# Feed-forward stages: block strides and reciprocals in PSUM, a shared bank, and the output product made later

## The chip, the cores and the metric

The kernel runs on one core of one Trainium2 chip. Times are microseconds of device time. A core has TensorE (PE, matrix products and transposes into PSUM), VectorE (DVE), ScalarE (ACT), GpSimd (POOL) and SyncE (SP), which issues DMAs. Each engine works its own list of instructions in order and waits on semaphores. PSUM has 8 banks of 512 float32 a partition here, and this stage uses them all.

## The reference

A network of two layers on 8 batches of 1024 tokens, 256 wide. Layer 0 is attention with relative positions, layer 1 is two Mamba layers, and each is followed by a feed-forward stage. The change touches only the two feed-forward stages, so this part of the reference matters:

```python
def fp4_quant_dequant(x):            # BLOCK = 16
    xb = x.reshape(shape[:-1] + (shape[-1] // BLOCK, BLOCK))
    scale = jnp.max(jnp.abs(xb), axis=-1, keepdims=True) / 6.0
    scale = jnp.maximum(scale, jnp.float32(1e-12))
    xn = xb / scale
    idx = jnp.searchsorted(_MID, jnp.abs(xn))
    q = _GRID[idx] * jnp.sign(xn) * scale
def fp4_linear(x, w):
    return jnp.einsum('bsk,nk->bsn', fp4_quant_dequant(x), fp4_quant_dequant(w))
gate = fp4_linear(x, w_gate)         # 256 -> 704
y = fp4_linear(x, w_up)
return fp4_linear(jax.nn.silu(gate) * y, w_down)   # 704 -> 256
...
h = _layernorm(x, axis=-1) * (1 + cb) + sb
x = x + gb * _L0_ffn_ref(h, L0_ffn_w_gate, L0_ffn_w_up, L0_ffn_w_down)
```

## The kernel before

`ffn_phase` (from L1298) does one feed-forward stage. It runs twice, over 64 tiles of 128 tokens each time. The quantised and turned weights stay in SBUF.

The loop is a software pipeline. `body(t, ...)` is called on every engine for t = n, and each part of it works on another tile: `early` on n+4 (mean and variance), `ahead` on n+3 (centering and modulation), `norm` on n+2 (rounding x to fp4), `turn` on n+1 (transpose of x, gate and up products), `middle` on n (h = silu(gate) * up, rounding h), `hturn` on n-1 (transpose of hq), `last` on n-2 (output product, gating, residual). The order of instructions on each engine is the order of the code in its body; no scheduler moves anything.

The names that matter, with their lines in the profile of before:

- TensorE, in this order: the output product into `out_ps` (L1673, six matmuls), two transposes of `xq` into `xT_ps` (L1682), six transposes of `hq` into `hT_ps` (L1692), eight gate and eight up matmuls into `gu_ps` (L1703). The transposes of `hq` wait for `s_hq`, which GpSimd raises.
- VectorE: `xamax` L1571, h L1578, `xstride` L1583, `hamax` L1587, `xinv` L1590, `hstride` L1593, `xq = xn * xinv` L1597, `xtmp` L1601, `hinv` L1604, statistics L1609, `hq = h * hinv` L1613, `htmp` L1622, the gating of the output L1627, then the four additions and subtractions that round: L1630 and L1632 on `xq`, L1635 and L1637 on `hq`.
- ScalarE: the copy of the turned x (L1739), centering (L1745), the masks' scaling (L1749, L1763), the copies of the turned `hq` (L1757, L1759), silu (L1770).
- GpSimd: modulation L1497 and L1503, `xscale` L1499, the residual add L1511, `hscale` L1513, the chain for the inverse deviation L1518, L1519, L1521, L1523, and last the scaling of `xq` and then `hq` by their block scales (both L118).

The strides and reciprocals (one number for each block of 16) lie in SBUF, `xT_ps` and `out_ps` have a PSUM bank each.

Of the kernel before, what the change touches and what calls it, by code (L numbers as in the profile page):

```python
# [15 lines left out]
P = 128  # L16
D = 256
# [10 lines left out]
FFN = 704  # L28
FC = -(-FFN // P)
BLOCK = 16  # L30
# [1267 lines left out]
def ffn_phase(nc, name, x_in, x_out, mods, w_gate, w_up, w_down, ident, batches):  # L1298
# [7 lines left out]
    with ExitStack() as ctx:  # L1306
        def sb(n, shape, dt=FP32):
            return ctx.enter_context(nc.sbuf_tensor(f"{name}_{n}", shape, dt))
# [44 lines left out]
        xq = sb("xq", [P, 2, D])  # L1353
        xtmp, htmp = sb("xtmp", [P, D]), sb("htmp", [P, FFN])
        xamax, hamax = sb("xamax", [P, 2, D // BLOCK]), sb("hamax", [P, 2, FFN // BLOCK])
        xstride, hstride = sb("xstride", [P, D // BLOCK]), sb("hstride", [P, FFN // BLOCK])
        xscale, hscale = sb("xscale", [P, D // BLOCK]), sb("hscale", [P, FFN // BLOCK])
        xinv, hinv = sb("xinv", [P, D // BLOCK]), sb("hinv", [P, FFN // BLOCK])
        xqT = sb("xqT", [P, 2, DC, P])
        gate = sb("gate", [P, 2, FFN])  # L1360
        h = sb("h", [P, FFN])
# [1 line left out]
        hqT = sb("hqT", [P, 2, FC, P])  # L1363
        res = sb("res", [P, 2, D])
        gu_ps = pb("gu_ps", [P, 4, BANK])
        xT_ps = pb("xT_ps", [P, BANK])
        hT_ps = pb("hT_ps", [P, 2 * BANK])
        out_ps = pb("out_ps", [P, BANK])

        turned_up = gu_ps[:, :, :].rearrange("p (c a) w -> p c (a w)", c=DC)  # L1370
        turned_down = gu_ps[:, 0:2, :].rearrange("p a w -> p (a w)")
# [268 lines left out]
        @block.tensor  # L1640
        def _(pe):
            def prepare(k):
                if k == 0:
                    return
                m = k - 1
                w = part(made, m)
                pe.wait_ge(s_wq, m + 1)
                ge(pe, s_wkept, m)
                if m < 2:
                    for c in range(FC):  # L1650
                        cw = min(P, FFN - c * P)
                        mm = nc.tensor.transpose(turned_down[0:cw, c * P:(c + 1) * P], w[:, c * P:c * P + cw], ident[:, :])
                elif m < 4:
                    for i in range(edge // P):
                        for c in range(DC):
                            mm = nc.tensor.transpose(turned_up[:, c, i * P:(i + 1) * P],
                                                     w[:, i * D + c * P:i * D + (c + 1) * P], ident[:, :])
                else:
                    for c in range(DC):
                        mm = nc.tensor.transpose(turned_up[:, c, 0:P], w[:, c * P:(c + 1) * P], ident[:, :])  # L1660
                mm.then_inc(s_wT, 1)
                if k == jobs:
                    pe.wait_ge(s_wkept, jobs)

            def body(t, early, ahead, norm, turn, middle, hturn, last):
                if last:
                    t0 = t.plus(-2)
                    k, u = t0.n, t0.u
                    pe.wait_ge(s_hqT, k + 1)
                    ge(pe, s_gated, k)  # L1670
                    for c in range(FC):
                        cw = min(P, FFN - c * P)
                        mm = nc.tensor.matmul(out_ps[:, 0:D], hqT[0:cw, u, c, :], wd[0:cw, c, :],  # L1673
                                              start=(c == 0), stop=(c == FC - 1))
                    mm.then_inc(s_out, 1)
                if turn:
                    t1 = t.plus(1)
                    k, u = t1.n, t1.u
                    pe.wait_ge(s_xq, k + 1)
                    ge(pe, s_xqT, k)  # L1680
                    for c in range(DC):
                        mm = nc.tensor.transpose(xT_ps[:, c * P:(c + 1) * P], xq[:, u, c * P:(c + 1) * P],  # L1682
                                                 ident[:, :])
                    mm.then_inc(s_xT, 1)
                if hturn:
                    t1 = t.plus(-1)
                    k, u = t1.n, t1.u
                    pe.wait_ge(s_hq, k + 1)
                    ge(pe, s_hqT, k)
                    for c in range(FC):  # L1690
                        cw = min(P, FFN - c * P)
                        mm = nc.tensor.transpose(hT_ps[0:cw, c * P:(c + 1) * P], hq[:, u, c * P:c * P + cw],  # L1692
                                                 ident[:, :])
                    mm.then_inc(s_hT, 1)
                if turn:
                    t1 = t.plus(1)
                    k, u = t1.n, t1.u
                    pe.wait_ge(s_xqT, k + 1)
                    ge(pe, s_h, k)
                    for w, at in ((wg, 0), (wu, 2)):  # L1700
                        for a in range(2):
                            for c in range(DC):
                                mm = nc.tensor.matmul(gu_ps[:, at + a, 0:HALF], xqT[:, u, c, :],  # L1703
                                                      w[:, c, a * HALF:(a + 1) * HALF],
                                                      start=(c == 0), stop=(c == DC - 1))
                        mm.then_inc(s_gate if at == 0 else s_gu, 1)
            run(pe, body, prepare)
# [831 lines left out]
```

## Time and profile before

| | |
|---|---|
| median of 3 runs | 9465.37 us (9464.44 to 9467.9) |
| the profiled execution | 9470.18 us, span 9468.5 us |
| the two feed-forward stages | about 3790 to 4430 us and 8790 to 9462 us of the span |
| steady part, TensorE / VectorE / GpSimd busy in 500 us | 475.8 / 494.3 / 425.9 us at a granted clock of 1.00 |

A stage begins with its weights and then settles to one tile after another. A row of a timeline or of the chain of waits shows the start in us from the start of the span, the duration in us, the engine, the line and what it writes and reads; in square brackets stands the idle time of the engine before it, and who ended it. A row of a line's durations shows the least, the median and the greatest in ns. Instructions of one engine overlap slightly at their ends, so the distance from start to start says more than the sum of durations.

### The profile page before, as it was taken

What the parts mean: (1) busy time and instruction counts of PE and PEld (TensorE: products, weight loads), DVE (VectorE), ACT (ScalarE), POOL (GpSimd) and SP (SyncE); (2) the same over time, 40 slices, a digit from 0 to 9 for tenths busy, and PEclk for the clock granted to TensorE, in tenths of its full rate; (3) what the DMA queues carried; (4) which work ended last, traced back from release to release, by engine and by line L of the source; (5) the groups of instructions that cost most, each with busy time, mean ns of one, the idle gap of its engine ahead of it and who ended that gap; (6) DMA issues with size and microseconds to landing.
All of it is one profiled execution on the core that took longest, in us unless ns stands there. A gap on an engine that the chain in (4) does not pass through costs nothing. (4 is left out here: it accounts for less than half of the span.)

```text
span 9468.5 us, 173659 instructions
## 1 busy us (share of the span) xinstructions
PE 8233.9 (87%) x48392; PEld 4721.2 (50%) x48392; DVE 8331.3 (88%) x12866; ACT 5642.4 (60%) x9235; POOL 5082.2 (54%) x4769
## 2 busy tenths in 40 slices
PE   6699999999999997897888888887788888888699
PEld 2366666666666666564333333333233333333466
DVE  5788888888888887997899999999699999999899
ACT  2377777777777775332666666665456656555333
POOL 1100000000000000785899999999699999999687
PEclk8799999999999999998999999999899999998899
DMA  7988888888888888111122111221222222211111
GB/s 236 306 272 281 282 280 283 281 281 279 282 283 281 280 280 267 46 43 47 77 82 82 72 56 77 82 82 44 94 80 72 76 91 91 91 68 71 53 43 40
DMA packets 1173912, 1447.40 MB, mean 153 GB/s; under 512 B 83402, under 2 KB 1053658, under 8 KB 1140736
## 3 DMA queue, kind: packets, MB, share of 16 engines
q1 hardware_dynamic: 1173568, 1444.18, 46.3%
q14 instruction: 295, 2.42, 0.1%
q8 instruction: 49, 0.80, 0.0%
HBM read 880.81 MB, written 564.60 MB: 153 GB/s over the span
## 5 line engine op out<-in xcount | busy, mean ns | idle before, releaser
L2109 POOL TENSOR_TENSOR mb_bx<-mb_dtu,mb_bc 128x512 f32<-128x512 f32 x2048 | 2662.0, 1324 | 13.7 <-DVE mb_hs L2209 13.2
L2352 PE MATMUL mb_y_ps<-mb_g,ident 128*128 128x512 f32 x4096 | 2187.1, 640 | 469.2 <-POOL mb_g L2116 235.0
L2396 ACT ACTIVATE mb_dA<-mb_dt,mb_a_neg 128x512 f32<-128x512 f32 x2048 | 1401.0, 688 | 1627.6 <-DVE mb_hs L2209 1084.9
L1471 POOL MEMSET f_magic<- 128x1 f32 x2 | 0.2, 98 | 3383.6 <-POOLq L127 3383.6
L2352 PEld LDWEIGHTS mb_y_ps<-mb_g,ident 128*128 128x128 f32 x4096 | 763.6, 199 | 1650.5 <-issue 729.0
L1017 ACT ACTIVATE at_tab<-at_e_ps 128x384 f32<-128x384 f32 x2064 | 1012.1, 490 | 790.1 <-PE at_e_ps L934 789.4
L1071 DVE TENSOR_REDUCE at_nmax<-at_s_ps 128x1 f32<-128x1024 f32 x1025 | 1255.2, 1225 | 35.1
L950 PE MATMUL at_pT_ps<-ident,at_probs 128*128 128x128 f32 x8192 | 1115.6, 279 | 101.8 <-ACT at_probs L1022 84.8
L1022 ACT ACTIVATE at_probs<-at_s_ps,at_nmax 128x1024 f32<-128x1024 f32 x1025 | 1140.8, 1113 | 62.5 <-DVE at_nmax L1071 39.0
L950 PEld LDWEIGHTS at_pT_ps<-ident,at_probs 128*128 128x128 f32 x8192 | 894.6, 141 | 403.2 <-ACT at_probs L1022 374.4
L2169 DVE TENSOR_TENSOR mb_g<-mb_hs,mb_bc 128x512 f32<-128x512 f32 x1472 | 993.7, 675 | 39.6 <-PE mb_y_ps L2352 38.3
L2209 DVE TENSOR_TENSOR_SCAN mb_hs<-mb_dA,mb_carry,mb_bx 128x512 f32<-128x512 f32 x736 | 935.4, 1283 | 98.0 <-POOL mb_bx L2109 38.2
L2209 DVE TENSOR_TENSOR_SCAN mb_hs<-mb_dA,mb_bx 128x512 f32<-128x512 f32 x736 | 896.5, 1224 | 77.2 <-POOL mb_bx L2109 38.1
L917 PE MATMUL at_s_ps<-at_opnd 105*128 105x512 bf16 (+3 forms) x2818 | 804.8, 326 | 9.2 <-DMA at_skew<-at_tables 8.8
L2116 POOL TENSOR_TENSOR mb_g<-mb_hs_sb,mb_bc 128x512 f32<-128x512 f32 x576 | 752.6, 1307 | 93.3 <-PE mb_y_ps L2352 85.3
L1069 DVE TENSOR_TENSOR at_s_ps<-at_s_ps,at_skew 128x384 f32<-128x384 f32 (+1 forms) x1025 | 542.8, 530 | 280.6 <-PE at_s_ps L921 157.1
L1076 DVE COPY at_probsT<-at_pT_ps 128x512 f32<-128x512 f32 x1024 | 697.0, 681 | 0.1
L969 PE MATMUL at_c_ps<-at_probsT,at_val 128*32 128x128 f32 x16384 | 659.7, 279 | 1.6 <-ACT at_probsT L1029 1.6
L921 PE MATMUL at_s_ps<-ident,at_skew 128*128 128x128 f32 x2818 | 609.2, 274 | 0.0
L2285 PE MATMUL mb_ring<-mb_xc,mb_diag 128*128 128x512 f32 x1024 | 522.7, 596 | 46.3 <-ACT mb_u L2449 43.7
L969 PEld LDWEIGHTS at_c_ps<-at_probsT,at_val 128*32 128x32 f32 x16384 | 384.9, 109 | 212.3 <-issue 202.0
L921 PEld LDWEIGHTS at_s_ps<-ident,at_skew 128*128 128x128 f32 x2818 | 392.4, 142 | 85.1 <-issue 0.4
(244 smaller groups left out, 14167.9 us busy)
## 6 DMA issues: line engine op xcount, KB each, us to landing
at_tables<-at_tab SPq DMA_DIRECT2D x1032, 384.0 KB, 4.0
at_skew<-at_tables SPq DMA_DIRECT2D x1030, 256.0 KB, 3.1
mb_bc<-mb_bc_rows SPq DMA_DIRECT2D x256, 1024.0 KB, 6.3
at_skew<-at_tables SPq DMA_DIRECT2D x773, 128.0 KB, 3.5
at_opnd<-at_q_st SPq DMA_DIRECT2D x130, 210.0 KB, 4.4
at_opnd<-at_kl_st SPq DMA_DIRECT2D x130, 210.0 KB, 4.7
at_opnd<-at_kr_st SPq DMA_DIRECT2D x130, 210.0 KB, 4.6
at_q_st<-st_parts SPq DMA_DIRECT2D x96, 256.0 KB, 4.1
```

The source lines that it names most:

```text
L917: mm = nc.tensor.matmul(s_ps[:, b, a * P:z * P], opnd[:, u, 0, q], opnd[:, u, side, a * P:z * P], start=True, stop=(len(near) == 0))
L921: mm = nc.tensor.matmul(s_ps[:, b, kt * P:(kt + 1) * P], skew[:, u, 1, kt, blk * P:(blk + 1) * P], ident[:, :], start=False, stop=(kt == n ...
L950: mm = nc.tensor.transpose(pT_ps[:, hb, k * P:(k + 1) * P], probs[:, i % 2, c:c + P], ident[:, :])
L969: mm = nc.tensor.matmul(c_ps[lane * VW:(lane + 1) * VW, q:q + P], val[:, h.u, k + lane, :], probsT[:, i0 % 2, (k + lane) * P:(k + lane + 1 ...
L1017: nc.scalar.activation(tab[:, e, :], e_ps[:, 0:BAND], ACT.Copy).then_inc(s_tab, 1)
L1022: nc.scalar.activation(probs[:, i % 2, :], s_ps[:, i % 2, :], ACT.Exp, bias=nmax[:, i % 2:i % 2 + 1], scale=1.0).then_inc(s_exp, 1)
L1071: nc.vector.tensor_reduce(nmax[:, b:b + 1], s_ps[:, b, :], axis=AX.X, op=ALU.max, negate=True).then_inc(s_max, 1)
L2109: pool.tensor_tensor(bx[:, s % RINGS, :], dtu[:, c, :], bc[:, 0, n, :], ALU.mult).then_inc(s_bx, 1)
L2169: nc.vector.tensor_tensor(g[:, s1 % RINGS, :], state(s1), bc[:, 1, n, :], ALU.mult).then_inc(s_g, 1)
L2209: nc.vector.tensor_tensor_scan(state(s), dA[:, s % DA_RING, :], bx[:, s % RINGS, :], initial=carry[:, s:s + 1] if k.u else 0.0, op0=ALU.mu ...
L2352: nc.tensor.matmul(y_ps[:, c % 2, :], ident[:, :], g[:, s1 % RINGS, :], start=False, stop=(n == STATE - 1)).then_inc(s_y, 1)
L2396: nc.scalar.activation(dA[:, s % DA_RING, :], dt[:, c, :], ACT.Exp, scale=a_neg[:, c, n:n + 1]).then_inc(s_dA, 1)
```

## The change

Three things change. The strides and reciprocals of the blocks of x and h move from SBUF to four quarters of a new PSUM bank, `blocks_ps`. To free that bank, `out_ps` and `xT_ps` become two halves of one bank, `out_xT_ps`, with two more waits that keep the engines from using both halves at once. And TensorE makes the output product behind the transposes of x and of `hq`, no longer ahead of them; the gate and up products stay behind it.

```diff
-        xstride, hstride = sb("xstride", [P, D // BLOCK]), sb("hstride", [P, FFN // BLOCK])
         xscale, hscale = sb("xscale", [P, D // BLOCK]), sb("hscale", [P, FFN // BLOCK])
-        xinv, hinv = sb("xinv", [P, D // BLOCK]), sb("hinv", [P, FFN // BLOCK])
...
-        xT_ps = pb("xT_ps", [P, BANK])
         hT_ps = pb("hT_ps", [P, 2 * BANK])
-        out_ps = pb("out_ps", [P, BANK])
+        out_xT_ps = pb("out_xT_ps", [P, BANK])
+        out_ps, xT_ps = out_xT_ps[:, 0:D], out_xT_ps[:, D:2 * D]
+        blocks_ps = pb("blocks_ps", [P, BANK])
+        xstride, xinv = (blocks_ps[:, i * BANK // 4:i * BANK // 4 + D // BLOCK] for i in (0, 1))
+        hstride, hinv = (blocks_ps[:, i * BANK // 4:i * BANK // 4 + FFN // BLOCK] for i in (2, 3))
...
             def body(t, early, ahead, norm, turn, middle, hturn, last):
-                if last:
-                    t0 = t.plus(-2)
-                    k, u = t0.n, t0.u
-                    pe.wait_ge(s_hqT, k + 1)
-                    ge(pe, s_gated, k)
-                    for c in range(FC):
-                        cw = min(P, FFN - c * P)
-                        mm = nc.tensor.matmul(out_ps[:, 0:D], hqT[0:cw, u, c, :], wd[0:cw, c, :],
-                                              start=(c == 0), stop=(c == FC - 1))
-                    mm.then_inc(s_out, 1)
                 if turn:
                     t1 = t.plus(1)
                     k, u = t1.n, t1.u
                     pe.wait_ge(s_xq, k + 1)
                     ge(pe, s_xqT, k)
+                    ge(pe, s_gated, k - 3)
...
                     mm.then_inc(s_hT, 1)
+                if last:
+                    t0 = t.plus(-2)
+                    k, u = t0.n, t0.u
+                    pe.wait_ge(s_hqT, k + 1)
+                    ge(pe, s_gated, k)
+                    if turn:
+                        pe.wait_ge(s_xqT, t.plus(1).n + 1)
+                    for c in range(FC):
+                        cw = min(P, FFN - c * P)
+                        mm = nc.tensor.matmul(out_ps[:, 0:D], hqT[0:cw, u, c, :], wd[0:cw, c, :],
+                                              start=(c == 0), stop=(c == FC - 1))
+                    mm.then_inc(s_out, 1)
```

TensorE's list for one tile in the loop of the first stage, before the change; a row shows the line, the operation, what it writes and reads, and the shape.

```order
L1673 MATMUL f_out_ps<-f_wd,f_hqT 128x256 x6
L1679 ISA
L1682 MATMUL f_xT_ps<-ident,f_xq 128x128 x2
L1692 MATMUL f_hT_ps<-ident,f_hq 128x128 x5
L1692 MATMUL f_hT_ps<-ident,f_hq 64x128
L1703 MATMUL f_gu_ps<-f_wg,f_xqT 128x352 x4
L1703 MATMUL f_gu_ps<-f_wu,f_xqT 128x352 x4
```

The same place after the change; L1696 is the output product, L1674 the transpose of x, L1684 that of `hq`.

```order
L1670 ISA
L41 REGISTER_ALU
L1674 MATMUL f_out_xT_ps<-ident,f_xq 128x128 x2
L1684 MATMUL f_hT_ps<-ident,f_hq 128x128 x5
L1684 MATMUL f_hT_ps<-ident,f_hq 64x128
L1696 MATMUL f_out_xT_ps<-f_wd,f_hqT 128x256 x6
L1707 MATMUL f_gu_ps<-f_wg,f_xqT 128x352 x4
L1707 MATMUL f_gu_ps<-f_wu,f_xqT 128x352 x4
```

The output product of tile n-2 now stands behind the transposes of `hq` of tile n-1. VectorE's list keeps its order; this is its piece from h to the reciprocals, before:

```order
L1578 TENSOR_TENSOR f_h<-f_gate,f_gu_ps 128x704
L69 ISA
L1583 TENSOR_SCALAR f_xstride<-f_xamax 128x16
L41 REGISTER_ALU
L1587 TENSOR_REDUCE f_hamax<-f_h 128x44
L69 REGISTER_ALU
L1590 RECIPROCAL f_xinv<-f_xstride 128x16
L69 ISA
L1593 TENSOR_SCALAR f_hstride<-f_hamax 128x44
L69 REGISTER_ALU
L1597 TENSOR_TENSOR f_xq<-f_xn,f_xinv 128x256
```

And after, where `f_blocks_ps` holds all four small arrays:

```order
L1579 TENSOR_TENSOR f_h<-f_gate,f_gu_ps 128x704
L69 ISA
L1584 TENSOR_SCALAR f_blocks_ps<-f_xamax 128x16
L41 REGISTER_ALU
L1588 TENSOR_REDUCE f_hamax<-f_h 128x44
L69 REGISTER_ALU
L1591 RECIPROCAL f_blocks_ps<-f_blocks_ps 128x16
L69 ISA
L1594 TENSOR_SCALAR f_blocks_ps<-f_hamax 128x44
L69 REGISTER_ALU
L1598 TENSOR_TENSOR f_xq<-f_xn,f_blocks_ps 128x256
```

Only the place of the operands has moved; GpSimd's and ScalarE's lists keep their order as well.

## Rows read from the trace of the kernel before

**Rows 1.** windows view, steady part of both stages: busy us (instructions) of each engine

```profile
core 0: us, PE busy (x) PEld busy (x) DVE busy (x) ACT busy (x) POOL busy (x), PEclk, DMA share, GB/s
3900.00:4400.00 500.00, 475.80 (x1957) 324.12 (x1958) 494.25 (x1030) 196.81 (x382) 425.88 (x592) 1.00 0.14 42
8900.00:9400.00 500.00, 475.14 (x1951) 323.26 (x1950) 494.15 (x1031) 196.90 (x380) 426.83 (x596) 1.00 0.14 43
```

**Rows 2.** chain of waits, second stage: start us, us, what

```profile
9044.53 0.38 PE f_xT_ps L1682 x2
...
9055.44 4.74 PE f_gu_ps L1703 x16
9060.18 2.79 PE f_out_ps L1673 x12
9062.96 0.38 PE f_xT_ps L1682 x2
```

**Rows 3.** timeline of one tile and the next, second stage

```profile
9057.16 0.42 DVE L1627 TENSOR_TENSOR f_res<-f_out_ps,f_mod 128x256 f32<-128x256 f32 x1
...
9057.50 0.54 DVE L1630 TENSOR_TENSOR f_xq<-f_xq,f_xtmp 128x256 f32<-128x256 f32 x1
...
9057.75 0.88 POOL L1511 TENSOR_TENSOR f_res<-f_res,f_xr 128x256 f32<-128x256 f32 x1
...
9058.08 0.83 DVE L1632 TENSOR_TENSOR f_xq<-f_xq,f_xtmp 128x256 f32<-128x256 f32 x1
...
9059.77 0.89 DVE L1637 TENSOR_TENSOR f_hq<-f_hq,f_htmp 128x704 f32<-128x704 f32 x1
...
9059.87 0.89 POOL L1519 TENSOR_SCALAR f_shift<-f_mean_var 128x1 f32<-128x1 f32 x1
...
9060.91 0.88 DVE L1578 TENSOR_TENSOR f_h<-f_gate,f_gu_ps 128x704 f32<-128x704 f32 x1
...
9063.56 0.88 PE L1692 MATMUL f_hT_ps<-ident,f_hq 128*128 128x128 f32 x6 [0.23 <-POOL f_hq L118]
...
9064.27 2.53 PE L1703 MATMUL f_gu_ps<-f_wg,f_xqT 128*128 128x352 f32 x8
...
9064.74 1.34 DVE L1613 TENSOR_TENSOR f_hq<-f_h,f_hinv 128x704 f32<-128x704 f32 x1
...
9066.56 0.42 DVE L1627 TENSOR_TENSOR f_res<-f_out_ps,f_mod 128x256 f32<-128x256 f32 x1
```

**Rows 4.** least/median/greatest ns of single lines over both stages

```profile
L1578 DVE TENSOR_TENSOR f_h<-f_gate,f_gu_ps x128: 870/876/889, 3834.6 to 9446.0; 128x704 f32<-128x704 f32 x128
L1583 DVE TENSOR_SCALAR f_xstride<-f_xamax x128: 168/453/517, 3812.7 to 9430.4; 128x16 f32<-128x16 f32 x128
L1593 DVE TENSOR_SCALAR f_hstride<-f_hamax x128: 135/484/490, 3836.5 to 9447.8; 128x44 f32<-128x44 f32 x128
L1613 DVE TENSOR_TENSOR f_hq<-f_h,f_hinv x128: 861/961/1350, 3837.9 to 9448.5; 128x704 f32<-128x704 f32 x128
L1518 POOL TENSOR_TENSOR f_rstd<-f_mean_var,f_eps x128: 185/575/578, 3797.1 to 9418.8; 128x1 f32<-128x1 f32 x128
L1519 POOL TENSOR_SCALAR f_shift<-f_mean_var x128: 233/887/889, 3797.3 to 9419.4; 128x1 f32<-128x1 f32 x128
```

**Rows 5.** timeline of the end of the second stage

```profile
9450.48 3.05 PE L1673 MATMUL f_out_ps<-f_wd,f_hqT 128*128 128x256 f32 x12 [0.95 <-ACT f_hqT L1759]
...
9453.57 0.42 DVE L1627 TENSOR_TENSOR f_res<-f_out_ps,f_mod 128x256 f32<-128x256 f32 x1 [0.52 <-PE f_out_ps L1673]
...
9454.63 0.88 PE L1692 MATMUL f_hT_ps<-ident,f_hq 128*128 128x128 f32 x6 [1.10 <-POOL f_hq L118]
...
9456.45 4.46 PE L1673 MATMUL f_out_ps<-f_wd,f_hqT 128*128 128x256 f32 x12 [0.95 <-ACT f_hqT L1759]
...
9460.95 0.42 DVE L1627 TENSOR_TENSOR f_res<-f_out_ps,f_mod 128x256 f32<-128x256 f32 x1 [6.96 <-PE f_out_ps L1673]
9461.46 0.72 POOL L1511 TENSOR_TENSOR f_res<-f_res,f_xr 128x256 f32<-128x256 f32 x1 [6.20 <-DVE f_res L1627]
```

## The prediction

> **What bounds the kernel now.** The change touches only the two feed-forward stages, so I first read the windows view over the steady part of each [rows 1]: in 500 us VectorE is busy 494 us, TensorE 475 to 476 us and GpSimd 426 us, at a granted clock of 1.00. All three are close to full, so busy shares don't say who leads. Then I read the chain of waits in the second stage [rows 2]. The reader is to see that it closes on itself: from one transpose of x at 9044.53 it runs through ScalarE and a long stretch of GpSimd that ends with the scaling of hq, back to TensorE's transposes of hq, gate and up products (9055.44), output product (9060.18) and the next transpose of x (9062.96). That is 18.43 us for two tiles, 9.215 us a tile. Last I read one tile in the timeline [rows 3] and the durations of single lines [rows 4], for who holds whom.
>
> Rows 3 and 4 show a second thing. VectorE's L1613 takes 0.87 us beside one tile and 1.34 us beside the next, with the same work. L1583 and L1593, on 16 and 44 elements, take 0.45 and 0.48 us as a median, and 0.17 and 0.135 us at least. GpSimd's L1518 and L1519, on one element a partition, take 0.58 and 0.89 us, and 0.19 and 0.23 us at least. In rows 3 L1519 starts 0.10 us after VectorE's L1637 starts and ends 0.10 us after it ends. So the two engines hold each other up where an instruction with two SBUF operands, or a plain copy-like one from SBUF to SBUF, meets a GpSimd one.
>
> **The change part by part.** Part one, strides and reciprocals in PSUM. In each tile four small instructions write PSUM, and L1597 and L1613 read their second operand there. Gain on VectorE [rows 4]: L1583 from 0.45 to 0.17 and L1593 from 0.48 to 0.135 us (0.28 and 0.35), L1613 from 1.34 or 0.87 to 0.87 (0.24 in the mean): 0.87 us of 9.215. What a PSUM operand costs is bounded by two rows of 704 elements: L1578, which reads PSUM, has a median of 0.876 us, and L1613, with both operands in SBUF, a minimum of 0.861. So about 0.01 us an instruction; I take that, and keep as the other end 0.1 us for each of the six, which would leave a gain of under 0.3. Taken alone, this part would relieve VectorE, which I price below as a rival.
>
> Behind these rows stands the Trainium skill, SBUF — State Buffer, section Who interferes with whom: a VectorE instruction with two SBUF inputs contends with a GpSimd instruction that reads SBUF, one with at most one SBUF input outside the two-port modes doesn't. By that rule the trace agrees: L1578, with one input in PSUM, stays within 0.870 to 0.889 us in all 128 tiles.
>
> Part two, the shared bank. The new waits are short. The transpose of x for tile n+1 waits for the gating L1627 of tile n-3, which was issued a tile ago. The output product waits for ScalarE's copy of the turned x, while six transposes of hq (0.71 us from their start to the next product's, rows 3) and the wait for hq lie between. I cost both at nothing; if that cover were gone they would cost a few tenths of a us.
>
> Part three, the move, decides. The output product of tile n-2 stood ahead of the transposes of hq of tile n-1, which wait for GpSimd's scaling; its 2.8 us [rows 2] ran while GpSimd was still working. Now it stands behind them. That closes a new ring, one tile long. GpSimd scales hq(n-1) at the end of its tile; TensorE turns it; only then comes the output product of n-2; VectorE gates it (L1627); GpSimd adds the residual (L1511), and only behind L1511 in its queue come L1513, L1518, L1519, L1521, L1523, the scaling of xq, and the scaling of hq(n). Queued behind the waiting transposes on TensorE are now the output product and all 16 gate and up products; behind L1627 on VectorE are L1630 to L1637, and behind L1511 seven GpSimd instructions.
>
> The ring's length, each step from a row:
> - start of the hq transposes to the start of the next product: 9064.27 less 9063.56 = 0.71 [rows 3];
> - start of the output product to the start of L1627 where VectorE waits for it: 9453.57 less 9450.48 = 3.09 [rows 5];
> - start of L1627 to the start of L1511 where GpSimd waits for it: 9461.46 less 9460.95 = 0.51 [rows 5];
> - start of L1511 to the start of the hq transposes: 9063.56 less 9057.75 = 5.81 [rows 3].
>
> Sum 10.12 us a tile, against 9.215: 0.905 us longer. In the last step GpSimd's durations are the contended ones. I keep them, because what contends there is L1630, L1632, L1635 and L1637, whose operands all stay in SBUF, and which follow L1627 on VectorE as L1511 follows it on GpSimd, so both start together as now. The floor of that step, with the least durations (L1511 0.72 for 0.88, rows 5 and 3; L1518 0.19 for 0.58 and L1519 0.23 for 0.89, rows 4; together 1.2 less), is 4.61 and the ring 8.92. Between 8.92 and 10.12 I take 10.12, the row of this very place.
>
> Is anything else later than the ring? With the hq transposes at 0, the output product runs from 0.71, L1627 from 3.80, the gate and up products from 3.50 (0.71 and the 2.79 that the product takes of TensorE's queue, rows 2) to 8.24 (4.74 long, rows 2). VectorE's h of the next tile starts at about 8.3. Now the start of h to that of L1627 takes 9066.56 less 9060.91 = 5.65 us in the tile where L1613 takes 1.34 [rows 3]; less 0.28, 0.35 and 0.47 that is 4.55, so VectorE is ready for the next L1627 at about 12.9, and the output product lets it go at 10.12 + 3.80 = 13.92. So VectorE has 1 us to spare, and the gain of part one, or an extra 0.1 us for PSUM operands, vanishes in it. TensorE's own work is 475.5 / 500 x 9.215 = 8.76 us a tile [rows 1], so it idles about 1.3 us a tile, waiting for hq.
>
> The sum over the kernel: the ring holds for tiles 2 to 59 of each stage (later ones lack L1518 to L1523, as nothing is left to normalise), 58 steps of 0.905 = 52.5 us. At the end of a stage the output product of tile 62 now lies between the last transposes of hq and the last output product: before, these start 1.82 us apart [rows 5], after it 0.71 + 2.79 = 3.50, so 1.7 us more. Together 54.2 us a stage, 108.4 for two. The profiled execution took 9470.18 us (span 9468.5), which gives 9578.6; the median of the runs shown is 9465.37, 4.8 lower, and by it the forecast is **9574 us**, 1.15% slower.
>
> **The rivals.**
> The first ends on the other side, faster. If GpSimd's stretch in the ring shrinks to its floor, because VectorE, idling before L1627 and freed by part one, no longer presses on it, the ring is 8.92. The old cycle of two tiles holds the same GpSimd instructions and shrinks by the same 1.2 us, to 17.2, or 8.6 a tile, and TensorE's own work is 8.76, so the ring still leads: 0.295 less on 116 tiles is 34 us, with 4 back for the ends about 9435. For it: three of VectorE's instructions do leave the contention. Against it: L1518 and L1519 lie beside L1635 and L1637, which don't change. It turns to a gain from where 0.9 of the 1.2 us is saved.
>
> The second is slower still: after L1627 VectorE issues L1630 and L1632 first, and L1511 gets through only behind both. Now L1630 starts 0.34 us after L1627 [rows 3]; two of 0.42, what L1627 takes for as many elements, end at 1.18, and L1511 starts there and not at 0.51: 0.67 more, 10.79 a tile, 1.575 x 116 + 4 = 187, or 9652. Against it: in rows 3 L1511 gets in between the two.
>
> The Trainium skill has a rule for this, in the same section of SBUF — State Buffer: not the kind of instruction but who issues first gets the shared ports. By that, idle engines released by the same event could go either way; no row here has GpSimd waiting for L1627 while VectorE has L1632 behind it.
>
> The third is no change that can be told: relief of about 0.9 of the 1.2 us, the ring at 9.2, about 9467.
>
> **How the numbers follow.** The forecast has 0.80, the slower rival 0.08, the faster one 0.07, no change 0.05. That is slower by over 0.2% 0.88, within 0.2% (about what runs of this kernel can tell) 0.05, faster 0.07. The range goes from a ring of 9.65, for which 0.47 of the 1.2 us is saved (0.435 x 116 + 4 = 54, about 9520), up to about the slower rival's time, 9650.
>
> **What would show it.** In the profile after: 20.2 us for two tiles in the steady part; TensorE waiting for hq about 1.3 us a tile, VectorE waiting before L1627 for the output product in nearly every tile, and GpSimd before L1511 for L1627, where now these waits occur only at the ends; the chain of waits running hq scaling, hq transposes, output product, gating, residual add. Busy time in 500 us would fall to about 433 us for TensorE (8.76 / 10.12) and 407 for VectorE (494.2 / 500 x 9.215 = 9.11, less 0.87, over 10.12), with L1583, L1593 and L1613 at about 0.18, 0.15 and 0.87 us. L1518 and L1519 would still be near 0.58 and 0.89. The prediction is wrong if these two fall to 0.2, if VectorE doesn't wait before L1627, or if the steady period is at or under 18.43 us for two tiles.

## The result, and the profile after

The changed kernel takes 9581.61 us as a median of 4 runs (9570.83 to 9587.66), against 9464.91 for the kernel before on the same chip (9463.94 to 9467.9): a ratio of 1.0118, with a 95% interval of 1.0105 to 1.0131. It is 1.2% slower. The profiled execution took 9580.14 us with a span of 9578.4, 109.9 longer than the span of before. The forecast was 9574 us, with 9520 to 9650 as its range.

Of the views that stand ahead of the prediction, these are the answers of the kernel after. First the windows view over the steady part of both stages, to be held against [rows 1]; the columns are the same.

```profile
3900.00:4400.00 500.00, 445.31 (x1782) 290.72 (x1782) 417.54 (x941) 186.69 (x348) 351.78 (x543) 1.00 0.12 39
8950.00:9450.00 500.00, 446.20 (x1781) 290.84 (x1780) 417.03 (x941) 186.72 (x347) 350.48 (x542) 1.00 0.12 39
```

No engine is close to full now, and TensorE's granted clock is still 1.00. So something that is no engine's busy time sets the pace. The timeline of two tiles in the second stage shows it, to be held against [rows 3]. The lines that concern us have moved by one: L1684 is the transposes of `hq`, L1696 the output product, L1628 the gating, L1512 the residual add.

```profile
9120.84 0.87 PE L1684 MATMUL f_hT_ps<-ident,f_hq 128*128 128x128 f32 x6 [0.81 <-POOL f_hq L118]
9121.55 2.95 PE L1696 MATMUL f_out_xT_ps<-f_wd,f_hqT 128*128 128x256 f32 x12
...
9124.81 0.42 DVE L1628 TENSOR_TENSOR f_res<-f_out_xT_ps,f_mod 128x256 f32<-128x256 f32 x1 [0.53 <-PE f_out_xT_ps L1696]
...
9125.40 0.75 POOL L1512 TENSOR_TENSOR f_res<-f_res,f_xr 128x256 f32<-128x256 f32 x1 [2.23 <-DVE f_res L1628]
...
9129.47 0.89 DVE L1579 TENSOR_TENSOR f_h<-f_gate,f_gu_ps 128x704 f32<-128x704 f32 x1 [0.95 <-PE f_gu_ps L1707]
...
9131.08 0.87 PE L1684 MATMUL f_hT_ps<-ident,f_hq 128*128 128x128 f32 x6 [0.84 <-POOL f_hq L118]
...
9134.77 0.42 DVE L1628 TENSOR_TENSOR f_res<-f_out_xT_ps,f_mod 128x256 f32<-128x256 f32 x1 [0.42 <-PE f_out_xT_ps L1696]
...
9135.27 0.84 POOL L1512 TENSOR_TENSOR f_res<-f_res,f_xr 128x256 f32<-128x256 f32 x1 [1.86 <-DVE f_res L1628]
...
9141.08 0.87 PE L1684 MATMUL f_hT_ps<-ident,f_hq 128*128 128x128 f32 x6 [0.81 <-POOL f_hq L118]
```

From one transpose of `hq` to the next but one it is 9141.08 less 9120.84 = 20.24 us for two tiles; before it was 18.43. Each of the four links of the ring can be read off: 0.71 from the transposes to the product, 3.26 from the product to the gating, 0.59 to the residual add, and 5.68 to the next transposes. The waits over 400 us of the second stage tell the same; the columns are the total in us, the number of waits, and the longest.

```profile
POOL f_res L1512 <- DVE f_res L1628: 81.5, 40, 2.2
...
DVE f_res L1628 <- PE f_out_xT_ps L1696: 18.8, 40, 0.5
```

In 40 tiles GpSimd waits 40 times for the gating, and VectorE 40 times for the output product. In the kernel before neither wait is in the list of this window. The chain of waits, whose run over the gating the prediction named as a sign, doesn't show the ring here: between 9120.84 and 9141.08 it goes over the output product, the gate and up products, h, and GpSimd's L1498 to L1504, and leaves the 1.82 us ahead of L1512 without a releaser. The timeline gives the same idle time (1.86 us) to the gating. So the ring is read from the waits in the timeline.

Last the least, median and greatest duration in ns of single lines, which answer to [rows 4]:

```profile
L1584 DVE TENSOR_SCALAR f_blocks_ps<-f_xamax x128: 163/171/178, 3809.9 to 9535.2; 128x16 f32<-128x16 f32 x128
L1594 DVE TENSOR_SCALAR f_blocks_ps<-f_hamax x128: 159/160/207, 3833.6 to 9554.6; 128x44 f32<-128x44 f32 x128
L1614 DVE TENSOR_TENSOR f_hq<-f_h,f_blocks_ps x128: 855/857/889, 3835.6 to 9555.3; 128x704 f32<-128x704 f32 x128
L1500 POOL TENSOR_SCALAR f_xscale<-f_xamax x128: 270/287/435, 3818.8 to 9534.7; 128x16 f32<-128x16 f32 x128
L1519 POOL TENSOR_TENSOR f_rstd<-f_mean_var,f_eps x128: 187/575/579, 3794.3 to 9521.4; 128x1 f32<-128x1 f32 x128
L1520 POOL TENSOR_SCALAR f_shift<-f_mean_var x128: 235/886/891, 3794.6 to 9522.1; 128x1 f32<-128x1 f32 x128
```

Against the kernel before, L1584 fell from 0.453 to 0.171 us, L1594 from 0.484 to 0.160, and L1614 varies by 0.03 us only. GpSimd gained too, which I had not priced: L1500, the scale of x, had a median of 0.808 us before and has 0.287 now. These differences hold both changes, the operands and the order; the first two experiments part them. L1519 and L1520 inside the ring stand where they stood.

The end of a stage answers to [rows 5]. This is the last part of the second stage in the timeline after:

```profile
9561.34 1.54 PE L1684 MATMUL f_hT_ps<-ident,f_hq 128*128 128x128 f32 x6 [5.15 <-POOL f_hq L118]
...
9562.68 4.57 PE L1696 MATMUL f_out_xT_ps<-f_wd,f_hqT 128*128 128x256 f32 x12
...
9567.85 3.02 PE L1696 MATMUL f_out_xT_ps<-f_wd,f_hqT 128*128 128x256 f32 x12 [0.61 <-DVE f_res L1628]
...
9570.91 0.42 DVE L1628 TENSOR_TENSOR f_res<-f_out_xT_ps,f_mod 128x256 f32<-128x256 f32 x1 [3.21 <-PE f_out_xT_ps L1696]
```

From the last transposes of `hq` to the last gating it takes 9.57 us, where it took 9460.95 less 9454.63 = 6.32 before.

### The profile page after: what moved, and what is told of

Same layout as the page of the kernel before. It is cut to its first block and busy times, and to the rows that moved or that the text cites. A ratio compares the mean times of both kernels' runs of the same rounds, so it can differ in the third digit from the quotient of the medians.

```text
span 9578.4 us, 173717 instructions
## 1 busy us (share of the span) xinstructions
PE 8259.7 (86%) x48392; PEld 4712.6 (49%) x48392; DVE 8253.0 (86%) x12866; ACT 5663.1 (59%) x9235; POOL 4988.9 (52%) x4769
```

## The experiments

### The move alone, and the move without the blocks in PSUM

The first kernel is the one before with nothing but the output product put behind the transposes of `hq`. Strides and reciprocals stay in SBUF, and `out_ps` and `xT_ps` keep their own banks.

```diff
-                if last:
-                    t0 = t.plus(-2)
...
-                    mm.then_inc(s_out, 1)
                 if turn:
...
                 if hturn:
...
+                if last:
+                    t0 = t.plus(-2)
...
+                    mm.then_inc(s_out, 1)
```

> Only the output product is moved behind the transposes of hq; strides and reciprocals stay in SBUF and every PSUM tile keeps its own bank. Ring theory (hq scaling, hq transposes, output product, gating, residual add, back to hq scaling, 10.12 us a tile): the same loss as the whole change, 9570 to 9600 us, about 20.2 us for two tiles, or up to 0.3 us a tile more, since the VectorE instructions that the PSUM operands relieved press again. Rival (the loss comes from the shared bank's waits or from PSUM operands): 9465 us, as before.

It took 9578.1 us (9572.1 to 9584.84, 4 runs) against 9464.19, a ratio of 1.0117 [1.0100, 1.0134]. A tile in its timeline:

```profile
9126.07 0.87 PE L1682 MATMUL f_hT_ps<-ident,f_hq 128*128 128x128 f32 x6 [0.91 <-POOL f_hq L118]
...
9136.30 0.87 PE L1682 MATMUL f_hT_ps<-ident,f_hq 128*128 128x128 f32 x6 [0.90 <-POOL f_hq L118]
```

This tile is 9136.30 less 9126.07 = 10.23 us long; the other of each pair is shorter, and two take 20.24 us. The move alone gives the whole loss. It also shortens instructions whose operands stay in SBUF, because they now meet other ones: L1613 has a median of 0.867 us for 0.961, L1593 0.232 for 0.484, and GpSimd's L1503 0.728 for 0.924. L1499 had 0.808 before; here it has

```profile
L1499 POOL TENSOR_SCALAR f_xscale<-f_xamax x128: 268/431/547, 3817.0 to 9539.9; 128x16 f32<-128x16 f32 x128
```

The second kernel is the one after with the strides and reciprocals back in SBUF.

```diff
-        blocks_ps = pb("blocks_ps", [P, BANK])
-        xstride, xinv = (blocks_ps[:, i * BANK // 4:i * BANK // 4 + D // BLOCK] for i in (0, 1))
-        hstride, hinv = (blocks_ps[:, i * BANK // 4:i * BANK // 4 + FFN // BLOCK] for i in (2, 3))
+        xstride, hstride = sb("xstride", [P, D // BLOCK]), sb("hstride", [P, FFN // BLOCK])
+        xinv, hinv = sb("xinv", [P, D // BLOCK]), sb("hinv", [P, FFN // BLOCK])
```

> The changed kernel with its strides and reciprocals back in SBUF; moved product and shared bank stay. Ring theory: VectorE has over 1 us a tile to spare, so what the PSUM operands save vanishes there: 9575 to 9600 us, against 9581.6 with them. Rival (PSUM operands cost time): 9540 us or less. Rival (they save time even here): 9620 us or more.

It took 9583.09 us (9574.23 to 9591.94, 4 runs), 1.0128 [1.0111, 1.0145]. So under this order the blocks in PSUM are worth nothing that can be measured, though they make VectorE's instructions shorter: against this kernel L1584 has 0.171 for 0.520 us and L1594 0.160 for 0.325 (medians). The shared bank costs nothing that can be measured either: this kernel has it and the first one doesn't.

### One suspected link made longer

If one link of a ring is made longer, what is added must come out whole in each tile. Here GpSimd makes one more product of 128x256 elements (0.72 us) just ahead of the scaling of xq, once in the kernel after and once in the one before.

```diff
+        extra = sb("extra", [P, D])
...
+                if middle and last:
+                    pool.tensor_tensor(extra[:, :], mod[:, 0, 0, :], mod[:, 0, 1, :], ALU.mult)
```

> The changed kernel with one more GpSimd instruction in each tile (128x256, two SBUF operands, about 0.75 us, its result unused) between L1524 and the scaling of xq. Ring theory: GpSimd's stretch from the residual add to the scaling of hq lies in a ring that is one tile long, so each tile gets the whole 0.7 to 0.8 us longer: 116 tiles x 0.75 = 87, 9655 to 9680 us. Rival (what bounds the tile lies on TensorE alone, in the shared bank or its waits, and GpSimd has 30% idle time): 9580 to 9600 us.

> The kernel before with the same extra GpSimd instruction in the same place. Theory: there GpSimd's stretch lies once in a cycle of two tiles, so a tile gets half of it longer, 0.37 us, as long as GpSimd's own sum (about 8.0 us busy, then 8.8) stays below: 9500 to 9520 us. Rival (a ring of one tile here too): 9550 us.

The kernel after took 9727.64 us (2 runs), 1.0269 [1.0248, 1.0289]. Where TensorE runs at full clock its tiles are 10.69 and 10.89 us long, 10.79 in the mean against 10.125: 0.66 of the 0.72. That is what the ring asks for. The rest of the time came from the clock. In its windows view, second stage, the granted clock is 0.90 (second column from the front is TensorE's busy time, the third number from the end the clock):

```profile
8950.00:9350.00 400.00, 310.40 (x1160) 202.91 (x1161) 306.46 (x656) 133.10 (x241) 258.51 (x405) 0.90 0.12 39
```

The output product took 4.49 us in a tile where part of it ran at 1.2 GHz, and 2.95 in the others, and that tile was 12.4 us long. So the mechanism held and the size was 50 us off.

The kernel before took 9570.25 us (2 runs), 1.0102 [1.0082, 1.0123]. That is more than twice the loss I had expected, and more than the rival's 9550 too. Most of its tiles are 9.64 and 10.42 us by turns:

```profile
9125.82 0.88 PE L1695 MATMUL f_hT_ps<-ident,f_hq 128*128 128x128 f32 x6 [0.91 <-POOL f_hq L118]
...
9135.46 0.88 PE L1695 MATMUL f_hT_ps<-ident,f_hq 128*128 128x128 f32 x6 [0.83 <-POOL f_hq L118]
...
9139.55 0.76 POOL L1512 TENSOR_TENSOR f_res<-f_res,f_xr 128x256 f32<-128x256 f32 x1 [1.88 <-DVE f_res L1630]
...
9145.88 0.88 PE L1695 MATMUL f_hT_ps<-ident,f_hq 128*128 128x128 f32 x6 [0.91 <-POOL f_hq L118]
```

The mean of 10.03 us is 0.82 longer than 9.215, so here as well the 0.72 us come out whole. This pair of kernels therefore doesn't tell a ring of one tile from the cycle of two; it shows only that GpSimd's stretch is in what sets the pace of both. The trace shows a way from GpSimd back to itself in the old order that I had not seen. VectorE's L1596 (L1593 in the kernel before), which takes the strides of h with their operands in SBUF, overlaps GpSimd's scaling of `hq` and ends about 0.04 us after it in 117 of its 128 runs, and in 116 of 128 in the kernel before. With the extra instruction its median is 1.06 us, where it was 0.484:

```profile
L1596 DVE TENSOR_SCALAR f_hstride<-f_hamax x128: 136/1061/1065, 3831.9 to 9542.4; 128x44 f32<-128x44 f32 x128
```

So a later GpSimd makes the rest of VectorE's list later, the gating with it, and GpSimd then waits for the gating (1.88 us in every second tile of the rows above). No kernel was run to test this way by itself.

### VectorE made longer, just ahead of the gating

One more VectorE instruction of 0.88 us ahead of the gating tells whether VectorE had room there: 1 us by the prediction in the kernel after, none in the one before.

```diff
+        extra = sb("extra", [P, FFN // BLOCK])
...
+                if middle and last:
+                    v.tensor_reduce(extra[:, :], blocks(h[:, :]), axis=AX.X, op=ALU.max, apply_absolute_value=True)
```

> The changed kernel with one more VectorE reduction in each tile (a copy of L1588, 704 elements, one SBUF operand, 0.89 us, its result unused), just ahead of the gating L1628. Ring theory: VectorE waits 0.95 to 1.23 us before h and 0.42 to 0.53 us before L1628 in each tile, and the extra instruction fills that: 9580 to 9610 us, at most 0.4 us a tile longer. Rival (VectorE is in what bounds the tile): 9680 us.

> The kernel before with one more VectorE reduction in each tile, the same copy of the hamax reduction (0.88 us, its result unused) just ahead of the gating that cost the changed kernel 16 us. Theory: before, VectorE is busy 9.11 of 9.215 us a tile and has nothing to spare, so the tile grows by 0.78 to 0.88 us: 116 tiles, 90 to 102 us, 9555 to 9570 us. Rival (VectorE's busy time is only waiting on the shared port and the cycle through GpSimd leads alone): 9465 to 9500 us.

In the kernel after: 9597.58 us (2 runs), 1.0131 [1.0111, 1.0152], two tiles in 20.53 us. Of 0.88 us only 0.14 a tile came out. In the kernel before: 9536.99 us (2 runs), 1.0076 [1.0056, 1.0096], tiles of 9.55 to 9.59 us at full clock, 0.35 longer, and stretches at a granted clock of 0.94. That lies between the times of the two theories. VectorE is nearly hidden in the kernel after and is not in the one before. But the room in the kernel after is not 1 us: there VectorE waits 0.53 and 0.42 us before L1628, and with the extra instruction it doesn't wait at all:

```profile
9124.94 0.88 DVE L1626 TENSOR_REDUCE f_extra<-f_h 128x44 f32<-128x704 f32 x1
9125.74 0.41 DVE L1631 TENSOR_TENSOR f_res<-f_out_xT_ps,f_mod 128x256 f32<-128x256 f32 x1
```

### The residual add taken out of the ring

If the ring were all, GpSimd's residual add could go behind the chain for the inverse deviation (L1518 to L1524), which doesn't need it. That shortens the ring by about 3 us, and the gain of the blocks in PSUM should show.

```diff
-                if last:
-                    k, u = t0.n, t0.u
-                    pool.wait_ge(s_gated, k + 1)
...
-                if middle:
-                    pool.tensor_scalar(hscale[:, :], hamax[:, t.u, :], 1.0 / 6.0, 1e-12, ALU.mult, ALU.max).then_inc(s_hscale, 1)
...
+                if middle:
+                    pool.tensor_scalar(hscale[:, :], hamax[:, t.u, :], 1.0 / 6.0, 1e-12, ALU.mult, ALU.max).then_inc(s_hscale, 1)
+                if last:
+                    k, u = t0.n, t0.u
+                    pool.wait_ge(s_gated, k + 1)
...
```

> The changed kernel with GpSimd's residual add put behind the short chain for the inverse deviation and hscale, just ahead of the scaling of xq. Ring theory: five instructions (about 3 us) leave the ring and run while GpSimd waits for the gating; what is left is the ring through VectorE (0.71 + 3.1 + 3.0 to 3.4 + 0.15 + 1.4 = 8.4 to 8.8) and TensorE's own 8.76 us, so 8.8 to 9.0 us a tile and 9415 to 9445 us. Rival (the moved product itself, the bank or a lower clock costs the time): no change from 9581 us.

It took 9588.23 us (9582.72 to 9596.18, 4 runs), 1.0128 [1.0111, 1.0145]: no gain in time. The chain of waits (start us, us, what) over two of its tiles, and the next two, shows what had been lying under the ring:

```profile
9120.54 0.87 PE f_hT_ps L1684 x6
9121.42 2.79 PE f_out_xT_ps L1696 x12
9124.20 4.95 PE f_gu_ps L1707 x16
...
9129.17 0.06 DVE f_h L1579
...
9133.86 0.18 DVE f_mean_var L1620
...
9139.03 1.35 POOL f_hq L118
...
9140.43 1.09 PE f_hT_ps L1684 x6
9141.52 4.25 PE f_out_xT_ps L1696 x12
...
9162.00 0.87 PE f_hT_ps L1684 x6
```

This is a second closed path, two tiles long: transposes of `hq`, output product, gate and up products, h, VectorE's chain, GpSimd's stretch, scaling of `hq`, transposes again. Here it is 9140.43 less 9120.54 = 19.89 us, which is 0.35 less than in the kernel after. The next two tiles take 9162.00 less 9140.43 = 21.57 us, because the output product ran in part at the lower clock (4.25 for 2.79 us; granted clock 0.70 from 9140.4 to 9146.0). Such tiles come again and again: the mean of two tiles is 20.4 us, so the clock took back a gain of some 20 us (0.17 us a tile on 116 tiles) and a little more. In the kernel after such a path, there by way of the gating, can be put together from the timeline above: 9120.84 to h at 9129.47, to VectorE being ready for the gating at 9134.77 less its wait of 0.42 = 9134.35, and from the gating to the transposes 6.31: 8.63 + 4.88 + 6.31 = 19.82 us for two tiles, against 20.24 for two rounds of the ring. The ring leads by 0.4 us for two tiles, and whatever shortens it alone gains no more than 0.2 us a tile. The extra VectorE instruction's 0.88 us on this path would make it 20.70; 20.53 was measured.

### The output product between the two transposes

```diff
                 if turn:
...
+                if last:
+                    t0 = t.plus(-2)
...
                 if hturn:
...
-                if last:
-                    t0 = t.plus(-2)
...
```

> The changed kernel with the output product between the two groups of transposes: behind those of x, ahead of those of hq. Shared bank, its waits and PSUM blocks stay. Ring theory: the product no longer waits for the scaling of hq, which GpSimd does last, but only for that of xq, 1.4 us earlier in its queue, and for ScalarE's copy of the turned x (about 1 us, with nothing to cover it now): 1.1 + 3.1 + 0.5 + 4.4 = 9.1 us a tile, so 9445 to 9480 us, the loss gone. Rival (the shared bank with its waits is what costs, or any place behind the transposes of x): 9560 us or more.

It took 9563.66 us (9557.57 to 9567.74, 4 runs), 1.0102 [1.0085, 1.0119]. The product no longer waits for `hq`, so the one-tile ring is gone, and yet 9147.20 less 9127.20 = 20.00 us pass for two tiles. Its chain of waits:

```profile
9127.20 0.45 PE f_out_xT_ps L1674 x2
...
9128.29 3.02 PE f_out_xT_ps L1686 x12
...
9132.11 4.75 PE f_gu_ps L1707 x16
...
9146.46 0.62 POOL f_xq L118
...
9147.20 0.45 PE f_out_xT_ps L1674 x2
```

A two-tile path again, 0.24 us shorter than in the kernel after. The product's 3.0 us stand between GpSimd's scaling (here that of xq) and the gate and up products. That is the time, and in part the reason, of the rival that takes any place behind the transposes of x. But 0.64 of the 20.00 us is TensorE's wait for ScalarE's copy of the turned x (from 9127.65 to 9128.29), and it is the shared bank that asks for this wait at this place. The same order with a bank for each was not run, so how much of the 20.00 is the place alone stays open. In the order of before the product stands ahead of the transposes of x too, and runs while GpSimd still scales.

### The output product last of all

```diff
-                if last:
-                    t0 = t.plus(-2)
...
                 if turn:
                     for w, at in ((wg, 0), (wu, 2)):
...
+                if last:
+                    t0 = t.plus(-2)
...
```

> The changed kernel with the output product one place later still, behind the 16 gate and up products. Ring theory: these 4.74 us then lie in the ring as well, 10.12 + 4.74 = 14.86 us a tile at full clock, 116 tiles x 5.65 = 655 us, 10120 us or more (more where TensorE's idle time lowers its clock). Rival (what counts is only that the product stands behind the waiting transposes, or the bank and the waits): 9560 to 9600 us.

It took 10424.29 us (2 runs), 1.1013 [1.0991, 1.1035]. The timeline and the windows view of the first stage:

```profile
4111.15 0.69 PE L1674 MATMUL f_out_xT_ps<-ident,f_xq 128*128 128x128 f32 x2 [5.09 <-POOL f_xq L118]
4112.39 1.54 PE L1684 MATMUL f_hT_ps<-ident,f_hq 128*128 128x128 f32 x6 [0.56 <-POOL f_hq L118]
4113.72 4.16 PE L1695 MATMUL f_gu_ps<-f_wg,f_xqT 128*128 128x352 f32 x8
4117.72 2.53 PE L1695 MATMUL f_gu_ps<-f_wu,f_xqT 128*128 128x352 f32 x8
```

```profile
3900.00:4400.00 500.00, 328.69 (x1050) 217.91 (x1048) 243.15 (x557) 106.01 (x203) 215.50 (x324) 0.80 0.07 23
```

The gate and up products have come into the ring: 10.12 + 4.74 [rows 2] is 14.86 us a tile. The tiles are 16.8 to 17.3 us long, since after each wait the transposes take 1.54 for 0.87 us and the gate products 4.16 for 2.53. So from the kernel after to this one the tile grows with the TensorE work between the scaling of `hq` and the output product's end, and by 2 us more for the clock.

### The old order with the blocks in PSUM

If the blocks' relief of VectorE was lost only because VectorE no longer led, it must show in the old order. There the bank has to come from elsewhere: `xT_ps` moves behind `hT_ps`'s 768 columns, into the second of its two banks.

```diff
+        hT_xT_ps = pb("hT_xT_ps", [P, 2 * BANK])
+        hT_ps, xT_ps = hT_xT_ps[:, 0:FC * P], hT_xT_ps[:, FC * P:FC * P + D]
+        blocks_ps = pb("blocks_ps", [P, BANK])
...
                 if turn:
...
+                    ge(pe, s_hqT, k - 2)
...
                 if hturn:
...
+                    if turn:
+                        pe.wait_ge(s_xqT, t.plus(1).n + 1)
```

> Before's order of TensorE, the strides and reciprocals in PSUM; the bank for them comes from letting the turned x share the second bank of the turned hq (two short waits). Theory: the port relief is worth something once no ring eats it. The cycle of two tiles loses what L1499 (0.81 to 0.28) and L1503 (0.92 to 0.73) lost, 18.43 to about 17.7, or 8.85 a tile, near TensorE's own 8.76: 9415 to 9435 us. Rival (PSUM operands bring nothing, or their access costs what the port gives): 9455 to 9480 us.

It took 9479.85 us (9472.92 to 9491.68, 10 runs), 1.0019 [1.0009, 1.0028]: no gain. In its timeline the added wait stands in every tile, because the transposes of `hq` follow at once on those of x, and ScalarE needs its time for the copy:

```profile
9129.93 0.44 PE L1684 MATMUL f_hT_xT_ps<-ident,f_xq 128*128 128x128 f32 x2
9130.94 0.85 PE L1696 MATMUL f_hT_xT_ps<-ident,f_hq 128*128 128x128 f32 x6 [0.56 <-ACT f_xqT L1743]
```

Only the fifth and sixth transposes write the shared bank. So in the next kernel the wait stands ahead of the fifth.

```diff
                     for c in range(FC):
                         cw = min(P, FFN - c * P)
+                        if turn and c == BANK // P:
+                            pe.wait_ge(s_xqT, t.plus(1).n + 1)
```

> The old order with PSUM blocks and the turned x in the second bank of the turned hq, but TensorE waits for ScalarE's copy of x only ahead of the fifth transpose of hq, the first that writes the shared bank. In the variant that waited ahead of the first one TensorE's own round was 2.88 + 1.09 + 0.68 + 4.73 = 9.38 us with 0.6 us of it waiting. Theory: four transposes now lie in that wait, 0.4 us a tile less, and then VectorE (9.05 us busy a tile there) or the cycle of two tiles (8.9) leads: 9435 to 9462 us, at or a little below the kernel before. Rival (the loss there was PSUM access cost or a tie with something else): 9475 to 9485 us as in that variant.

It took **9434.96 us** (9429.15 to 9443.43, 4 runs) against 9472.5 for the kernel before, 0.9958 [0.9941, 0.9974]: faster than both kernels. The tile shown takes 9136.70 less 9127.76 = 8.94 us, two take 17.87 for 18.43 before, and the wait for the copy is gone:

```profile
9127.76 0.88 PE L1696 MATMUL f_hT_xT_ps<-ident,f_hq 128*128 128x128 f32 x6 [0.16 <-POOL f_hq L118]
...
9136.70 0.88 PE L1696 MATMUL f_hT_xT_ps<-ident,f_hq 128*128 128x128 f32 x6 [0.18 <-POOL f_hq L118]
```

```profile
8950.00:9350.00 400.00, 392.63 (x1611) 267.32 (x1610) 394.64 (x849) 163.36 (x313) 329.78 (x495) 1.00 0.14 44
```

Both TensorE and VectorE are busy over 98% of the time. A tile is 9.215 less 8.93 = 0.28 us shorter than before, which on some 120 tiles is 34 of the 37.5 us. Its chain of waits closes over two tiles through GpSimd as that of before does [rows 2], and GpSimd's L1500 in it has a median of 0.442 us for 0.808, its L1504 0.730 for 0.924: 0.56 us together, as much as the two tiles lost. So the relief by the blocks in PSUM is real in the old order, and in the kernel with the early wait that wait hid it.

The Trainium skill, PSUM — Partial Sum Buffer, section PSUM bank collisions raise a hardware error, asks for semaphores by bank and not by address. What the two kernels add is the price of its place: waits of 0.56 to 0.64 us a tile ahead of the first transpose, which made the tile 0.41 us longer (9.34 for 8.93), and nothing that can be seen in the steady tiles ahead of the first one that writes the bank.

## Why the prediction was right, and where it fell short

**The ring.** It was forecast at 10.12 us a tile and came out at 10.125 in the mean. The links, of two tiles next to each other: 0.71 was 0.71 and 0.70; 3.09 was 3.26 and 2.99; 0.51 was 0.59 and 0.50; 5.81 was 5.68 and 5.81. All four had been measured in the kernel before at places where the same engines waited in the same order, and that is why the sum held. The first kernel of the experiments shows that the move alone is the cause. The product at the very end shows on a larger scale that what is put into the ring comes out of it. The extra GpSimd instruction came out too, but it did so in the old order as well, so it is no proof of the ring by itself.

**The contended durations.** I kept L1518 at 0.58 and L1519 at 0.89 us, because their neighbours on VectorE don't change. They measured 0.575 and 0.886. The rival of a faster kernel needed them at 0.19 and 0.23, and it is out. So is the rival in which GpSimd is held back behind two VectorE additions: L1512 started 0.59 us after the gating, and the second of them, L1633, only after 0.79 us.

**The shared bank at nothing.** Right, by the first two experiments.

**The blocks in PSUM.** VectorE's own work fell from 9.11 us a tile to 417.3 / 500 x 10.125 = 8.45, by 0.66, where I had 0.87. And only part of it belongs to the blocks: the kernel with the new order and the blocks in SBUF has 435.1 / 500 x 10.145 = 8.83, so the operands gave 0.38 and the new order the other 0.28. My 0.87 took each contended duration for a matter of the operands alone. A PSUM operand costs L1598 0.421 for 0.411 us and each reciprocal on x 0.255 for 0.236, about the 0.01 us that I took. It all went into VectorE's waits, as forecast. TensorE was busy 446 us in 500 and not 433.

**What was missing.** The step "is anything else later than the ring?" was wrong in its size and in what it concluded. VectorE was to be ready for the gating 12.9 us after the transposes of `hq`, with 1 us to spare. It was ready after 9134.35 less 9120.84 = 13.51. Half of the difference is on TensorE: the gate and up products ended at 8.60 and not at 8.24, since the transposes took 0.87 of its queue where I had 0.71, and the 16 products 4.94 where I had 4.74 (chain of waits of the kernel after, same tile, to be held against [rows 2]):

```profile
9120.84 0.87 PE f_hT_ps L1684 x6
...
9124.50 4.94 PE f_gu_ps L1707 x16
```

The other half is on VectorE: 4.88 us from h to the gating and not 4.55, with L1584 and L1614 already counted as short. And this chain closes on itself over two tiles at 19.82 us, which I never added up. It didn't change the forecast, as 20.24 is longer. It did change what I took for a remedy: two of my expectations, for the residual add moved later and for the product between the transposes, were built on the ring alone, and missed by 143 and 84 us from their upper ends; in the first of them the lower clock had its part too. The prediction was right about what leads and silent about what comes 2% behind it.

**The ends of the stages.** This is the term that was sized wrong: I had 1.7 us a stage. From its first transposes of `hq` to its last gating the first stage takes 640.4 for 581.1 us and the second 640.9 for 583.5, so 59.4 and 57.5 us more, 116.8 in all, where I had 108.4. Fifty-eight steps of 0.91 are 52.8 of each; the ends are the other 6.6 and 4.7. In the second stage 9.57 less 6.32 = 3.25 of it comes behind the last transposes: TensorE runs them and a part of the output product at its lower clock (1.54 for 0.88, 4.57 for 2.95), and the last product also waits 0.61 us for the gating. The medians differ by 116.7 us. In the two profiled executions it is 109.9, because what lies outside these two stretches took 6.9 us less in the one of the kernel after; nothing was changed there, so that the 109.9 comes so close to 108.4 is luck.

**The rival of no change** had 0.9 of the 1.2 us of contention relieved. Inside the ring only L1512 became shorter, 0.754 for 0.905 us as a median, and it did so with the order alone too (0.753). GpSimd's other gains, 0.5 us in L1500 and 0.2 in L1504 (0.924 to 0.729), stand ahead of L1512, where GpSimd waits 1.9 to 2.2 us a tile for the gating, and most of them came with the order: by itself it gave 0.431 and 0.728. What the operands did is told by two kernels of one order. With the blocks in SBUF L1613 takes up to 1.00 us and L1499 has a median of 0.432; with them in PSUM it is 0.889 at most, and 0.287. The Trainium skill, SBUF — State Buffer, section Who interferes with whom, makes the contention a matter of pairs, a VectorE instruction with two SBUF inputs against a GpSimd one that reads SBUF, and these two kernels agree with it.

## What to carry to other kernels

In a software pipeline over engines with fixed orders, look for every closed path through the orders, add each up from rows where the engines wait for one another, and divide by the number of tiles that it spans: the longest sets the pace, and the second longest says what a remedy can give. Two engines that hold each other up make such a link as well, without any semaphore. A product whose inputs have long been there belongs ahead of an instruction that waits for a slow engine, in the time in which that engine still works. Where a shared bank needs a wait, put it ahead of the first instruction that touches the bank, not ahead of the group.

## What the runs showed of the hardware that I had not expected

- TensorE's granted clock, 1.00 in the steady part of the kernels before and after, fell in some of the kernels with longer waits: to 0.97 over 500 us of the kernel with the residual add later, to 0.90 in the window shown of the kernel after with the extra GpSimd instruction, to 0.80 where the product came last. After waits of 5.09 and 0.56 us the six transposes and most of the gate products ran at 1.2 GHz and the up products behind them at 2.4 GHz again. A change that makes TensorE wait can so cost more than its ring. The kernel before with the extra VectorE instruction had stretches at 0.94 too. Why there and not in the kernel after was not tried.
- Small VectorE instructions that write PSUM take about what they take in SBUF without a neighbour: 0.171 and 0.160 us with 16 and 44 elements, where the least in SBUF was 0.168 and 0.135 [rows 4]. In SBUF, in the kernel before, they took 0.45 to 0.48 as a median, and the one on 44 elements ended with GpSimd's scaling of `hq` (0.04 us behind it in 116 of 128 cases).
- Contention works both ways: GpSimd's scale of x, on 16 elements, went from 0.432 to 0.287 us when only VectorE's small arrays had moved to PSUM (new order), and from 0.808 to 0.442 in the old order.
